# Attention on one core: scores and probabilities of two sequences in one step, and later products with v

## The chip, the core and the metric

The kernel runs on one core of a Trainium2 chip, in one launch. TensorE multiplies a stationary operand by a moving one into PSUM (eight banks of 128 partitions x 512 fp32), VectorE (DVE), ScalarE (ACT) and GpSimd (POOL) work beside it, and SyncE starts the DMAs. Each engine goes through its own queue in order and waits on semaphores. The metric is device time in microseconds. The kernel before takes 2264.89 us, the median of three runs (2263.42 to 2267.68).

## The reference

Four layers with residuals run over 16 sequences of 256 tokens, width 256: attention, a mixture of 16 experts (two per token) with shared ones, a state-space layer, a second mixture. Each layer's input and output are normalised, and the result is added to x. Only attention matters here. It has 16 query heads and 4 key/value heads of width 16, so that four query heads share one key head:

```
q = rope((x @ Wq.T + bq));  k = rope((x @ Wk.T + bk));  v = x @ Wv.T + bv
scores = q . k * 16**-0.5, causal mask
attended = softmax(scores) @ v
out = attended @ Wo.T + bo
```

All of it is fp32.

## The kernel before, in words

The kernel's parts follow each other: attention for all 16 sequences, then the first mixture, then a tail of state-space layer and second mixture. In attention a sequence is two tiles of 128 tokens. Key head g lies in partitions 32g to 32g+15 (a slot of 32, `SLOT`), so the products of different key heads use different groups of 32 rows of TensorE's array.

Scores are computed twice. In `scores`, queries are the stationary operand and keys are the moving one; VectorE takes each query's negated maximum from PSUM (line 1325) and writes it beside q as a seventeenth column. q with that column is transposed again (`turn_m`), and in `probs` the keys are stationary and 4 x 128 queries move: this gives scores less their maximum, keys on partitions. ScalarE takes the exponential (line 1251). In `av` the v of one key head, with a column of ones for the sum, is stationary with 32 columns, and lands in partitions 32g to 32g+31 of bank 4 or 5. ScalarE copies this (`copy_av`), TensorE turns it (`turn_av`), VectorE divides (`att`), TensorE turns (`turn_att`) and multiplies with Wo (`proj`), and VectorE adds the bias, normalises and adds to x (`post`, line 1343).

Each of scores, probs and av is cut into six units (`unit(i)`, line 1036): a pair of key heads, by query tile and key tile, (0,0), (1,0), (1,1). Scores of query tile 1 see both key tiles in one unit, so a score unit has eight products of 128 keys or four of 256. A mask comes first into the same bank, as a bf16 product with all 128 rows (lines 1141 and 1171). Unit i of scores and of probs uses banks 0 and 1 or 2 and 3, by its heads; they alternate. An fp32 product shows as two records, one for each of its two passes.

The order is written out by hand: `ORDER` (line 1044) lists steps as (sequence ahead, step, index), and every engine goes through the same list by `go_through` (line 57) and does what is its own in each step. Bank 6 serves x, q-k-v and the turned output, bank 7 q and k, bank 4 the output product as well. On VectorE, `norm` waits for GpSimd's power of -0.5 (line 1393) and then normalises x itself (line 1290); `rope` (line 1293) reads q-k-v from PSUM with the bias, rotates, writes q in four adds (line 1315) and copies v (line 1319).

Line 1752 (ScalarE, scale and shift by column operands, 128x256) and line 1950 (GpSimd, 128x512 sum in fp32) are of the tail and serve as measures.

Of the kernel before, what the change touches and what calls it, by code (L numbers as in the profile page):

```python
# [16 lines left out]
ALU = mybir.AluOpType  # L17
# [3 lines left out]
P = 128  # L21
# [892 lines left out]
class Attention:  # L914
# [8 lines left out]
    def __init__(self, k, a):  # L923
# [18 lines left out]
        self.qm_ready = k.sem("attn_qm_ready")  # L942
# [28 lines left out]
    def buffers(self, sb):  # L971
# [22 lines left out]
        self.probs = sb("probs", [P, 2, SEQ_TILES, REP, P])  # L994
# [33 lines left out]
SEQS = B  # L1028
# [7 lines left out]
def unit(i):  # L1036
# [17 lines left out]
def attention_order(t, par, first, last):  # L1054
    for ahead, what, i in ORDER:
        if not (ahead == -1 and first or ahead == 1 and last):
            yield what, t + ahead, (par + ahead) % 2, i


def attention_head(self):  # L1060
    for what, i in (("norm", 0), ("turn_x", 0), ("qkv", 0), ("rope", 0), ("qkv", 1), ("rope", 1),
                    ("turn_q", 0), ("turn_q", 1), ("turn_k", 0)):
        yield what, 0, 0, i
    yield from attention_order(0, 0, True, False)
    yield from attention_order(1, 1, False, False)


def attention_pair(self, it):
    yield from attention_order(2 * it + 2, 0, False, False)
    yield from attention_order(2 * it + 3, 1, False, False)  # L1070


def attention_rest(self):
    yield from attention_order(SEQS - 2, 0, False, False)
    yield from attention_order(SEQS - 1, 1, False, True)
    for what, i in (("turn_av", 1), ("att", 0), ("turn_att", 0), ("proj", 0), ("post", 0)):
        yield what, SEQS - 1, 1, i
# [3 lines left out]
Attention.turns = (SEQS - 4) // 2  # L1081
# [3 lines left out]
def is_last(t, n):  # L1085
    return isinstance(t, int) and t == n - 1


def attention_tensor(k, m, pe):
    nc = k.nc  # L1090

    def step(what, t, par, i):
        qb, half, heads = unit(i)
        if what == "turn_x":
            pe.wait_ge(m.xn_ready, t + 1)
            if begun(t - 1):
                pe.wait_ge(m.attT_ready, t - 1)
            for c in range(KD):
                for j in range(SEQ_TILES):
                    last = nc.tensor.transpose(k.bank[:, 6, (c * SEQ_TILES + j) * P:(c * SEQ_TILES + j + 1) * P],  # L1100
                                               m.xn[:, j, c * P:(c + 1) * P], k.ident[:])
            last.then_inc(m.xT_full, 1)
        if what == "qkv":
            pe.wait_ge(m.xT_ready, t + 1)
            if begun(2 * t + i):
                pe.wait_ge(m.qkv_read, 2 * t + i)
            for c in range(KD):
                last = nc.tensor.matmul(k.bank[:, 6, 0:NQKV], m.xT[:, c, i * P:(i + 1) * P], m.w_qkv[:, c, :],  # L1108
                                        start=(c == 0), stop=(c == KD - 1))
            last.then_inc(m.qkv_full, 1)  # L1110
        if what == "turn_q":
            pe.wait_ge(m.rope_ready, 2 * t + i + 1)
            if i == 0:
                if begun(2 * t):
                    pe.wait_ge(m.qmT_ready, 2 * t)
            else:
                pe.wait_ge(m.qkv_read, 2 * t + 2)
            for r in range(REP):
                last = nc.tensor.transpose(k.bank[:, 7 - i, r * P:(r + 1) * P],
# [1254 lines left out]
```

## Time and profile before

| | |
|---|---|
| median of three runs | 2264.89 us |
| the profiled execution's own time | 2262.32 us |
| its span | 2260.5 us |
| TensorE busy | 2044.2 us, 90% |
| VectorE, ScalarE, GpSimd busy | 1316.9, 740.8, 306.3 us |
| mean granted clock of TensorE | 0.944 |

Busy time of an engine is the time in which it executes something; matmuls are pipelined and their ends are modelled, so the distance from one start to the next says more than a duration. The granted clock is 1.00 at 2.4 GHz and 0.50 at 1.2 GHz; a mean between them says that part of the stretch ran at either. "Idle before" is the time an engine stood still before an instruction, with what ended it. A few matmul records are missing from a trace.

### The profile page before, as it was taken

The page shows a single profiled execution, that of the slowest core. Times are in us where ns is not written, and L with a number is a line of the kernel's source. Part 1 is how long each engine was busy: PE and PEld are TensorE (multiplying, and loading weights), DVE is VectorE, ACT ScalarE, POOL GpSimd, SP SyncE. Part 2 cuts the span into 40 slices and gives each one's busy share as a digit, 9 for nine tenths or more (in the row PEclk, how much of TensorE's full clock was granted, in tenths as well). Part 3 has the DMA queues.
Part 4 walks back from the last instruction along what each step waited for, and adds up shares of the span by engine and source line. Part 5 has one row for each costly group of instructions (what it writes and reads, how often), then busy time and mean ns, then how long its engine had stood idle before and what let it go on. Part 6 is the DMA issues. An engine that isn't in the chain of part 4 may idle for free.

```text
span 2260.5 us, 34928 instructions
## 1 busy us (share of the span) xinstructions
PE 2044.2 (90%) x10162; PEld 1455.7 (64%) x10211; DVE 1316.9 (58%) x3916; ACT 740.8 (33%) x1495; POOL 306.3 (14%) x459
## 2 busy tenths in 40 slices
PE   7999999997689888885579999999999999999998
PEld 3544454443667655553367887778777787777887
DVE  3565655553533222223667777777777777777653
ACT  1233323332234322322433443334333343333321
POOL 1000000001055333333000010011100011000000
PEclk7899989988599999998779999999999999999999
DMA  9800000000022222223111101111011110111100
GB/s 347 159 1 0 0 0 0 0 0 1 0 81 93 76 77 77 74 77 143 66 52 52 57 6 56 56 52 56 5 56 56 52 45 16 56 56 38 43 20 32
DMA packets 75462, 120.74 MB, mean 53 GB/s; under 512 B 18420, under 2 KB 59508, under 8 KB 74868
## 3 DMA queue, kind: packets, MB, share of 16 engines
q1 hardware_dynamic: 68468, 100.93, 14.1%
q0 software_dynamic: 6912, 18.92, 2.3%
q8 instruction: 28, 0.46, 0.1%
q14 instruction: 54, 0.44, 0.1%
HBM read 81.73 MB, written 38.08 MB: 53 GB/s over the span
## 4 chain that ended last, share of the span: by engine, by line
PE 77%; DVE 9%; issue 6%; DMA 4%; ACT 3%; POOL 1%; SPq 0%; DVEq 0%; POOLq 0%; ACTq 0%
PE bank L184 20%; PE bank L193 10%; PE bank L1146 5%; PE bank L1175 5%; DMA moe_rows<-sorted_in 3%; PE bank L561 3%; PE bank L1185 3%; PE bank L617 2%; PE bank L1624 2%; PE bank L1108 2%; DVE conv L1845 2%; PE bank L579 2%; PE bank L637 2%; PE bank L524 2%; PE bank L1212 2%
## 5 line engine op out<-in xcount | busy, mean ns | idle before, releaser
L184 PE MATMUL bank<-moe_xT,up_w 128*128 128x256 f32 x2304 | 552.3, 383 | 0.0
L184 PEld LDWEIGHTS bank<-moe_xT,up_w 128*128 128x128 f32 x2304 | 433.9, 190 | 69.7 <-issue 11.4
L193 PE MATMUL bank<-down_w,moe_hT 128*128 128x256 f32 x1152 | 306.5, 389 | 34.0 <-ACT moe_y L230 18.4
L227 ACT ACTIVATE moe_silu<-bank 128x256 f32<-128x256 f32 x288 | 110.7, 384 | 636.2 <-PE bank L184 636.2
L193 PEld LDWEIGHTS bank<-down_w,moe_hT 128*128 128x128 f32 x1152 | 203.9, 190 | 74.2 <-issue 28.8
L1325 DVE TENSOR_REDUCE q_slots<-bank 128x4 f32<-128x1024 f32 (+1 forms) x96 | 116.3, 1221 | 124.9 <-PE bank L1146 124.9
L1251 ACT ACTIVATE probs<-bank 128x1024 f32<-128x1024 f32 x96 | 98.4, 1025 | 201.8 <-PE bank L1175 201.8
L617 PE MATMUL bank<-up_w,moe_xT 128*128 x320 | 114.5, 481 | 25.9 <-issue 25.3
L1146 PE MATMUL bank<-kT,qT 16*128 16x256 f32 (+1 forms) x1024 | 124.9, 376 | 0.0
L1866 DVE TENSOR_TENSOR_SCAN m<-bank,delta 128x256 f32<-128x256 f32 x128 | 86.6, 676 | 61.8 <-PE bank L1663 60.5
L824 DVE TENSOR_TENSOR moe_h<-moe_silu,bank 128x176 f32<-128x176 f32 x80 | 27.0, 337 | 152.6 <-ACT moe_silu L696 149.9
L294 DVE TENSOR_TENSOR moe_hT<-moe_silu,bank 128x256 f32<-128x256 f32 x256 | 107.7, 421 | 8.8
L1175 PE MATMUL bank<-qmT,kT 17*128 17x512 f32 x384 | 110.9, 654 | 0.0
L293 DVE TENSOR_TENSOR moe_silu<-moe_silu,up_w 128x256 f32<-128x256 f32 x192 | 81.1, 422 | 43.3 <-ACT moe_silu L227 37.4
L1146 PEld LDWEIGHTS bank<-kT,qT 16*128 16x128 f32 x1024 | 83.3, 204 | 35.0 <-issue 30.1
L637 PE MATMUL bank<-down_w,moe_hT 88*128 x320 | 89.3, 401 | 0.6 <-ACT moe_hT L701 0.6
L561 PE MATMUL bank<-up_w,moe_xT 128*128 128x352 f32 x256 | 88.4, 469 | 0.9 <-issue 0.5
L617 PEld LDWEIGHTS bank<-up_w,moe_xT 128*128 128x128 f32 x320 | 55.6, 194 | 51.8 <-issue 35.4
L868 POOL DMA_INDIRECT results<-moe_result,moe_home x80 | 79.4, 993 | 20.1 <-POOL pool_spare L867 14.9
L326 POOL TENSOR_TENSOR moe_prstd<-moe_pmv,minus_half 128x2 f32<-128x2 f32 x16 | 12.4, 773 | 514.0 <-DVE moe_pmv L304 514.0
L1845 DVE SCALAR_TENSOR_TENSOR conv<-feat,taps,conv 128x256 f32<-128x256 f32 x192 | 80.0, 478 | 0.6
L1185 PE MATMUL bank<-probs,v_slots 128*32 128x512 f32 x384 | 75.8, 606 | 0.3
(293 smaller groups left out, 3226.9 us busy)
## 6 DMA issues: line engine op xcount, KB each, us to landing
up_w<-comb_rows SPq DMA_DIRECT2D x32, 768.0 KB, 5.2
comb_got<-results SPq DMA_DIRECT2D x16, 768.0 KB, 7.8
moe_rows<-sorted_in SPq DMA_DIRECT2D x80, 128.5 KB
sorted_in<-zero SPq DMA_DIRECT2D x10, 1024.0 KB, 10.3
down_w<-comb_rows SPq DMA_DIRECT2D x16, 512.0 KB, 7.6
up_w<-in_up SPq DMA_DIRECT2D x2, 3168.0 KB, 14.5
up_w<-in_up SPq DMA_DIRECT2D x2, 2304.0 KB, 13.0
results<-moe_y SPq DMA_DIRECT2D x32, 128.0 KB
```

Of the source, the lines that this page charges most:

```text
L184: last = mm(k.bank[:, UP_BANK + i % 3, half * S:(half + 1) * S], m.w_up[:, c, at + half * m.inter:at + (half + 1) * m.inter], m.xT[:, par, ...
L193: last = mm(k.bank[:, SUM_BANK, j * D:(j + 1) * D], m.hT[:, i % 3, j * P:(j + 1) * P], m.w_down[:, m.expert(i), :], start=(i == 0 and j == ...
L227: nc.scalar.activation(m.silu[:, i % 3, :], k.bank[:, UP_BANK + i % 3, 0:S], ACT.Silu).then_inc(m.silu_ready, 1)
L294: tt(m.hT[:, i % 3, :], m.silu[:, i % 3, :], u, ALU.mult).then_inc(m.h_ready, 1)
L561: last = nc.tensor.matmul(k.bank[:, 2 + i, 0:2 * inter], m.xT[:, par, c, :], m.w_up[:, c, lo:lo + 2 * inter], start=(c == 0), stop=(c == K ...
L617: last = nc.tensor.matmul(k.bank[:, 2 + par, 0:2 * inter], m.xT[:, par, c, :], cols(m.w_up[:, c, :], expert, 2 * inter), start=(c == 0), s ...
L637: last = nc.tensor.matmul(k.bank[:, 6 + par, 0:D], m.hT[0:m.half, par, c, :], w_down[0:m.half, bass.ds(expert * 2 * D + c * D, D)], start= ...
L1146: last = nc.tensor.matmul(x[:, r, :], m.qT[rows, par, qb, half * per + r, :], m.kT[rows, par, 0:keys], start=False, stop=(r == per - 1), s ...
L1175: last = nc.tensor.matmul(k.bank[:, g, :], m.kT[rows, par, half * P:(half + 1) * P], m.qmT[rows, qb].rearrange("p r n -> p (r n)"), start= ...
L1185: last = nc.tensor.matmul(k.bank[OW * g:OW * (g + 1), 4 + qb, :], m.v[:, par, half, g, :], m.probs[:, i % 2, g % PAIR].rearrange("p r n -> ...
L1325: v.tensor_reduce(m.q[:, par, qb, half * per:(half + 1) * per, heads[0]:heads[0] + PAIR, HD].rearrange("p r g -> p g r"), k.bank[:, heads[ ...
L1845: last = stt(dst, src[:, i:i + S], taps[:, i:i + 1], dst, ALU.mult, ALU.add)
```

## The change

One step, `pair`, takes the place of `scores` and `probs`. In period t it does score unit i of sequence t+1 and probability unit i^1 of sequence t, so the two use different pairs of key heads and with them different groups of rows. Masks of both come first; then products alternate, score and probability, until the probability's two are issued, and the rest of the scores follow. Scores always use banks 0 and 1, probabilities 2 and 3, and the next `pair` waits for the maximum (`max_ready`) and the exponential (`probs_ready`) of the one before. `probs` has four buffers instead of two.

`av` has three steps of four products, two units each, one step after their exponentials; the third comes in the next period. q-k-v is computed two sequences ahead, x is normalised three ahead. The bias add with the read of PSUM is a step of its own (`read`), ahead of the rotation (`rope`). Bank 6 now takes the output product too, and each of banks 6 and 7 is used for one thing at a time, with waits for its last reader. ScalarE normalises x (`xn`) and the output (`z`) by scale and shift and copies v (`copy_v`); GpSimd computes the shift with two small instructions and adds the output to x (`add`); VectorE takes that sum's statistics in a later step (`stat`). VectorE writes q by one add over all heads, and divides in one instruction per tile. The loop runs over (16 - 6) / 2 turns of two periods, with three periods and the preparation of sequences 0 and 1 ahead of it and six behind.

```diff
-        self.probs = sb("probs", [P, 2, SEQ_TILES, REP, P])
+        self.probs = sb("probs", [P, 4, PAIR, REP, P])
+        self.shift = sb("attn_shift", [P, SEQ_TILES])
+        self.pshift = sb("attn_pshift", [P, SEQ_TILES])
...
+SCORE_BANK, PROB_BANK, AV_BANK, MIX_BANK, TURN_Q_BANK = 0, 2, 4, 6, 7
 ORDER = (
-    (0, "scores", 0), (0, "scores", 1), (0, "scores", 2), (0, "turn_m", 0), (-1, "att", 0), (-1, "turn_av", 1),
-    (0, "scores", 3), (0, "scores", 4), (-1, "turn_att", 0), (1, "norm", 0), (0, "scores", 5), (-1, "proj", 0),
-    (0, "probs", 0), (-1, "post", 0), (1, "turn_x", 0), (0, "probs", 1), (0, "turn_m", 1), (1, "qkv", 0),
-    (0, "av", 0), (0, "probs", 2), (1, "rope", 0), (0, "av", 1), (0, "copy_av", 0), (0, "probs", 3), (1, "qkv", 1),
-    (0, "av", 2), (0, "av", 3), (0, "probs", 4), (0, "turn_av", 0), (1, "rope", 1), (1, "turn_q", 0), (0, "probs", 5),
-    (1, "turn_k", 0), (1, "turn_q", 1), (0, "av", 4), (0, "av", 5), (0, "copy_av", 1),
+    (0, "pair", 0), (1, "scores", 0), (0, "probs", 0), (1, "copy_v", 0), (3, "norm", 0), (-1, "av", 2), (-1, "copy_av", 1),
+    (0, "turn_m", 1), (2, "qkv", 0), (2, "read", 0),
+    (0, "pair", 1), (1, "scores", 1), (0, "probs", 1), (-1, "turn_av", 1), (-1, "att", 0), (3, "xn", 0), (2, "qkv", 1),
+    (2, "read", 1), (-2, "z", 0), (-2, "add", 0),
+    (0, "pair", 2), (1, "scores", 2), (0, "probs", 2), (0, "av", 0), (0, "copy_av", 0), (-1, "turn_att", 0), (1, "turn_m", 0),
+    (2, "rope", 0),
+    (0, "pair", 3), (1, "scores", 3), (0, "probs", 3), (0, "turn_av", 0), (3, "turn_x", 0), (2, "turn_q", 0), (2, "rope", 1),
+    (0, "pair", 4), (1, "scores", 4), (0, "probs", 4), (0, "av", 1), (2, "turn_q", 1), (-2, "stat", 0),
+    (0, "pair", 5), (1, "scores", 5), (0, "probs", 5), (-1, "proj", 0), (-1, "post", 0), (2, "turn_k", 0),
...
+def attention_period(t, par):
     for ahead, what, i in ORDER:
-        if not (ahead == -1 and first or ahead == 1 and last):
+        here = (0, 1) if what == "pair" else (ahead,)
+        if not isinstance(t, int) or any(0 <= t + a < SEQS for a in here):
             yield what, t + ahead, (par + ahead) % 2, i
...
+        if what == "pair":
+            scores, probs = within(t + 1), within(t)
+            if scores:
+                s, its = t + 1, (par + 1) % 2
+                qb, half, heads = unit(i)
+                keys, per = (qb + 1) * P, REP // (qb + 1)
+                pe.wait_ge(m.qT_ready, 2 * s + qb + 1)
+                pe.wait_ge(m.kT_ready, s + 1)
+                if begun(UNITS * s + i):
+                    pe.wait_ge(m.max_ready, UNITS * s + i)
+                for n in range(PAIR):
+                    x = k.bank[:, SCORE_BANK + n, :].rearrange("p (r n) -> p r n", r=per)
+                    mm(x[:, :, keys - P:keys], k.ident_b[:], m.mask_q[:, 0:per, :], start=True, stop=False,
+                       skip_group_check=True)
+            if probs:
+                pqb, phalf, pheads = unit(i ^ 1)
+                masked = phalf == pqb
+                pe.wait_ge(m.qmT_ready, 2 * t + pqb + 1)
+                if begun(UNITS * t + i):
+                    pe.wait_ge(m.probs_ready, UNITS * t + i)
+                if masked:
+                    for n in range(PAIR):
+                        mm(k.bank[:, PROB_BANK + n, :], k.ident_b[:], m.mask_k[:].rearrange("p r n -> p (r n)"),
+                           start=True, stop=False, skip_group_check=True)
+            for n in range(PAIR * REP):
+                r, lane = divmod(n, PAIR)
+                if scores and r < per:
+                    rows = slice(SLOT * heads[lane], SLOT * heads[lane] + HD)
+                    last = mm(k.bank[:, SCORE_BANK + lane, r * keys:(r + 1) * keys], m.qT[rows, its, qb, half * per + r, :],
+                              m.kT[rows, its, 0:keys], start=False, stop=(r == per - 1), skip_group_check=True)
+                    if n == PAIR * per - 1:
+                        last.then_inc(m.scores_full, 1)
+                if probs and r == 0:
+                    rows = slice(SLOT * pheads[lane], SLOT * pheads[lane] + HD + 1)
+                    last = mm(k.bank[:, PROB_BANK + lane, :], m.kT[rows, par, phalf * P:(phalf + 1) * P],
+                              m.qmT[rows, pqb].rearrange("p r n -> p (r n)"), start=not masked, stop=True,
+                              skip_group_check=True)
+                    if lane == PAIR - 1:
+                        last.then_inc(m.probs_full, 1)
...
+            pe.wait_ge(m.probs_ready, UNITS * t + PAIR * i + PAIR)
+            qb, half, _ = unit(PAIR * i)
             if i == 0:
+                pe.wait_ge(m.v_ready, t + 1)
                 if begun(t):
-                    pe.wait_ge(m.proj_used, t)
-            for g in heads:
-                last = nc.tensor.matmul(k.bank[OW * g:OW * (g + 1), 4 + qb, :], m.v[:, par, half, g, :],
-                                        m.probs[:, i % 2, g % PAIR].rearrange("p r n -> p (r n)"),
-                                        start=(half == 0), stop=(half == qb), skip_group_check=True)
+                    pe.wait_ge(m.att_ready, t)
+            for u in (PAIR * i, PAIR * i + 1):
+                for g in unit(u)[2]:
+                    last = mm(k.bank[OW * g:OW * (g + 1), AV_BANK + qb, :], m.v[:, par, half, g, :],
+                              m.probs[:, ((u ^ 1) + 2 * par) % 4, g % PAIR].rearrange("p r n -> p (r n)"),
+                              start=(half == 0), stop=(half == qb), skip_group_check=True)
             last.then_inc(m.probs_used, 1)
...
+        if what == "xn":
+            act.wait_ge(m.rstd_ready, t + 1)
+            if begun(t):
+                act.wait_ge(m.xT_full, t)
+            for j in range(SEQ_TILES):
+                last = activation(m.xn[:, j, :], cols(k.x, SEQ_TILES * t + j), ACT.Identity, bias=m.shift[:, j:j + 1],
+                                  scale=m.rstd[:, j:j + 1])
+            last.then_inc(m.xn_ready, 1)
...
+        if what == "read":
+            dve.wait_ge(m.qkv_full, 2 * t + i + 1)
+            if i == 0 and begun(t):
+                dve.wait_ge(m.v_ready, t)
+            v.tensor_tensor(m.qkv[:, i, :], k.bank[:, MIX_BANK, 0:NQKV], m.b_qkv[:], ALU.add).then_inc(m.qkv_read, 1)
...
-            for g in range(KV):
-                sl = slice(g * REP * HD, (g + 1) * REP * HD)
-                v.tensor_tensor(m.q[:, par, i, :, g, 0:HD], m.rot_a[:, sl].rearrange("p (r f) -> p r f", r=REP),
-                                m.rot_b[:, sl].rearrange("p (r f) -> p r f", r=REP), ALU.add)
+            v.tensor_tensor(m.q[:, par, i, :, :, 0:HD].rearrange("p r g f -> p g r f"),
+                            m.rot_a[:, 0:NQ].rearrange("p (g r f) -> p g r f", g=KV, r=REP),
+                            m.rot_b[:, 0:NQ].rearrange("p (g r f) -> p g r f", g=KV, r=REP), ALU.add)
             v.tensor_tensor(m.kk[:, i, :, 0:HD], m.rot_a[:, NQ:NQK].rearrange("p (g f) -> p g f", g=KV),
-                            m.rot_b[:, NQ:NQK].rearrange("p (g f) -> p g f", g=KV), ALU.add)
-            v.tensor_copy(m.v[:, par, i, :, 0:HD], m.qkv[:, i, NQK:NQKV].rearrange("p (g f) -> p g f", g=KV))\
-                .then_inc(m.rope_ready, 1)
+                            m.rot_b[:, NQ:NQK].rearrange("p (g f) -> p g f", g=KV), ALU.add).then_inc(m.rope_ready, 1)
...
+        if what == "add":
+            pool.wait_ge(m.z_ready, t + 1)
+            x = cols(k.x, t, SEQ_TILES * D)
+            g.tensor_tensor(x, x, m.y[:].rearrange("p j d -> p (j d)"), ALU.add).then_inc(m.x_done, 1)
```

## Rows read from the trace of the kernel before

**Rows 1.** The page's first block: busy time, share, instructions of each engine

```profile
PE 2044.2 (90%) x10162; PEld 1455.7 (64%) x10211; DVE 1316.9 (58%) x3916; ACT 740.8 (33%) x1495; POOL 306.3 (14%) x459
```

**Rows 2.** Windows: us, busy (count) per engine, clock, DMA, GB/s

```profile
24.30:64.10 39.80, 39.31 (x164) 18.31 (x166) 13.85 (x34) 9.78 (x13) 0.70 (x1) 0.66 1.07 338
...
139.66:170.09 30.43, 30.06 (x181) 14.99 (x183) 18.82 (x57) 10.77 (x15) 1.39 (x2) 1.00 0.00 1
...
291.80:326.01 34.21, 33.84 (x181) 17.06 (x183) 19.43 (x57) 10.77 (x15) 1.39 (x2) 0.88 0.00 0
326.01:360.67 34.66, 34.12 (x181) 17.30 (x183) 18.89 (x56) 10.77 (x15) 1.39 (x2) 0.87 0.00 0
```

**Rows 3.** Timeline, TensorE, 170 to 202: start us, us, line, count, idle

```profile
171.96 1.99 PE L1212 MATMUL bank<-w_o,attT 128*128 128x256 f32 x8
...
177.45 0.66 PE L1157 MATMUL bank<-ident,q_slots 128*128 128x128 f32 x4
177.94 1.46 PE L1108 MATMUL bank<-w_qkv,attn_xT 128*128 128x384 f32 x4
179.33 1.05 PE L1185 MATMUL bank<-probs,v_slots 128*32 128x512 f32 x4
180.31 1.13 PE L1175 MATMUL bank<-qmT,kT 17*128 17x512 f32 x4
...
184.89 1.07 PE L1185 MATMUL bank<-probs,v_slots 128*32 128x512 f32 x8
186.12 0.38 PE L1171 MATMUL bank<-mask_k,ident_b 128*128 128x512 bf16 x1 [0.16 <-issue]
...
188.42 0.59 PE L1171 MATMUL bank<-mask_k,ident_b 128*128 128x512 bf16 x2
188.94 1.13 PE L1175 MATMUL bank<-qmT,kT 17*128 17x512 f32 x4
190.00 0.44 PE L1126 MATMUL bank<-ident,k_slots 128*128 128x128 f32 x2
...
190.80 1.44 PE L1185 MATMUL bank<-probs,v_slots 128*32 128x512 f32 x8
192.18 0.60 PE L1141 MATMUL bank<-mask_q,ident_b 128*128 128x512 bf16 x2
...
194.34 1.16 PE L1146 MATMUL bank<-kT,qT 16*128 16x128 f32 x16
195.43 0.39 PE L1141 MATMUL bank<-mask_q,ident_b 128*128 128x256 bf16 x2
195.75 1.13 PE L1146 MATMUL bank<-kT,qT 16*128 16x256 f32 x8
196.83 0.66 PE L1157 MATMUL bank<-ident,q_slots 128*128 128x128 f32 x4
```

**Rows 4.** Groups of VectorE, 170.09 to 200.52: count, busy us, mean ns, idle

```profile
L1325 DVE TENSOR_REDUCE q_slots<-bank 128x4 f32<-128x1024 f32 x5 | 6.0, 1216 | 0.2 <-PE bank L1146 0.2
...
L1315 DVE TENSOR_TENSOR q_slots<-rot_a,rot_b 128x64 f32<-128x64 f32 x8 | 1.3, 220 | 0.1
...
L1358 DVE TENSOR_SCALAR attn_y<-attn_y,attn_pmv,attn_prstd 128x256 f32<-128x256 f32 x2 | 0.7, 412 | 0.8 <-POOL attn_prstd L1396 0.8
```

**Rows 5.** Groups of ScalarE, same stretch; last row whole span

```profile
L1251 ACT ACTIVATE probs<-bank 128x1024 f32<-128x1024 f32 x6 | 6.1, 1024 | 11.4 <-PE bank L1175 11.4
...
L1752 ACT ACTIVATE conv<-feat,taps 128x256 f32<-128x256 f32 x64 | 33.0, 589 | 0.0
```

**Rows 6.** Groups of GpSimd, whole span

```profile
L1950 POOL TENSOR_TENSOR down_w<-down_w 128x512 f32<-128x512 f32 x16 | 20.2, 1264 | 254.7 <-ACT down_w L1771 254.7
```

**Rows 7.** Timeline, TensorE, 314 to 320

```profile
314.42 1.16 PE L1146 MATMUL bank<-kT,qT 16*128 16x128 f32 x16
...
317.46 1.74 PE L1146 MATMUL bank<-kT,qT 16*128 16x256 f32 x8
```

**Rows 8.** Timeline, all engines, the stage's start

```profile
23.79 0.59 PE L1141 MATMUL bank<-mask_q,ident_b 128*128 128x512 bf16 x2 [0.82 <-ACT kT L1239]
```

**Rows 9.** Timeline, all engines, the stage's end

```profile
554.30 0.22 DVE L712 TENSOR_TENSOR moe_diff<-next_stat 128x32 f32<-128x32 f32 x1
```

More of the change, by code:

```diff
@@ L1051 @@
 )
-def attention_order(t, par, first, last):
+def attention_period(t, par):
     for ahead, what, i in ORDER:
-        if not (ahead == -1 and first or ahead == 1 and last):
+        here = (0, 1) if what == "pair" else (ahead,)
+        if not isinstance(t, int) or any(0 <= t + a < SEQS for a in here):
             yield what, t + ahead, (par + ahead) % 2, i
 def attention_head(self):
[L1061 to L1065, printed above, removed]
+    for s in (0, 1):
+        for what, i in (("norm", 0), ("xn", 0), ("turn_x", 0)):
+            yield what, s, s, i
+        if s == 0:
+            for what, i in (("qkv", 0), ("read", 0), ("qkv", 1), ("read", 1), ("rope", 0), ("rope", 1), ("turn_q", 0), ("turn_q", 1), ("turn_k", 0)):
+                yield what, s, s, i
+    for t in (-1, 0, 1):
+        yield from attention_period(t, t % 2)
@@ L1080, with within @@
 Attention.head, Attention.pair, Attention.rest = attention_head, attention_pair, attention_rest
-Attention.turns = (SEQS - 4) // 2
+Attention.turns = (SEQS - 6) // 2
 Attention.finished = SEQS
-def is_last(t, n):
-    return isinstance(t, int) and t == n - 1
+def within(t):
+    return not isinstance(t, int) or 0 <= t < SEQS
 def attention_tensor(k, m, pe):
     nc = k.nc
+    mm, turn = nc.tensor.matmul, nc.tensor.transpose
     def step(what, t, par, i):
-        qb, half, heads = unit(i)
+        mix, turned = k.bank[:, MIX_BANK, :], k.bank[:, TURN_Q_BANK, :]
@@ L1152, in step @@
             if i == 0:
-                pe.wait_ge(m.kT_ready, t + 1)
+                if begun(t):
+                    pe.wait_ge(m.qmT_ready, 2 * t)
+                else:
+                    pe.wait_ge(m.kT_ready, 1)
             else:
                 pe.wait_ge(m.qmT_ready, 2 * t + 1)
+                if within(t + 1):
+                    pe.wait_ge(m.kT_ready, t + 2)
             for r in range(REP):
-                last = nc.tensor.transpose(k.bank[:, 7, r * P:(r + 1) * P],
-                                           m.q[:, par, i, r].rearrange("p g s -> p (g s)"), k.ident[:])
+                last = turn(turned[:, r * P:(r + 1) * P], m.q[:, par, i, r].rearrange("p g s -> p (g s)"), k.ident[:])
@@ L1192, in step @@
             for r in range(REP):
-                last = nc.tensor.transpose(k.bank[:, 4 + i, r * P:(r + 1) * P], m.avT[:, i, r, :], k.ident[:])
+                last = turn(k.bank[:, AV_BANK + i, r * P:(r + 1) * P], m.avT[:, i, r, :], k.ident[:])
             last.then_inc(m.av_turned, 1)
@@ L1262, in step @@
                 act.wait_ge(m.proj_full, t)
-            nc.scalar.copy(m.attT[:].rearrange("p c t -> p (c t)"), k.bank[:, 6, :]).then_inc(m.attT_ready, 1)
+            copy(m.attT[:].rearrange("p c t -> p (c t)"), mix).then_inc(m.attT_ready, 1)
+        if what == "z":
+            act.wait_ge(m.post_rstd, t + 1)
+            for j in range(SEQ_TILES):
+                last = activation(m.y[:, j, :], m.y[:, j, :], ACT.Identity, bias=m.pshift[:, j:j + 1],
+                                  scale=m.prstd[:, j:j + 1])
+            last.then_inc(m.z_ready, 1)
     go_through(m, act, step)
```

206 lines of the change are left out of this document (84 added, 122 removed).

## The prediction

> **What bounds the kernel now.** I read the page's first block, then a table of stretches, one for each sequence of the attention stage, then TensorE's timeline inside one sequence, then the groups of the other engines there. TensorE is busy for 90% of the span [rows 1]. The change touches only the attention stage, which ends where the expert layer's first vector instruction starts, at 554.30 us [rows 9]. In the stretches the reader is to see that one sequence takes 30.43 us at full clock, that TensorE is busy in 30.06 of them, and that VectorE has 18.82 and ScalarE 10.77 [rows 2]. So TensorE's order of work alone sets the pace, and sixteen sequences of it are the stage.
>
> What fills it is in the timeline. I use start to start, since shown durations overlap. A probability product (two heads, 17 rows of the array each, 512 columns) takes 188.94 to 190.00 = 1.06 us. A score product (two heads, 16 rows each) takes 1.09 or 1.08 us, 128 or 256 keys wide [rows 3]. Two row groups of four work in each, the other two idle. With v, two column groups work in the first unit's product: 179.33 to 180.31, 0.98. The row at 184.89 shows eight records, two units at once in four column groups. The next row starts 1.23 later, but it holds one mask where there are two, a record is missing; less one mask (0.215) the four groups took about 1.0, as two do. So one pass over the array costs about 1.05 us however many groups are in it; for columns the trace shows that, for four row groups it doesn't.
>
> The clock is the second cost. The sequences that start at 291.80 and 326.01 took 34.21 and 34.66 instead of 30.43, with a granted clock of 0.88 and 0.87 [rows 2]: together 8.0 us. The two from 421.52 lose the same 8 (34.24, 34.64 in the same view). Before the first fall the engine did the two 128-key score products with their masks, only 16-row work; the fall shows as 1.74 for a group [rows 7] that takes 1.13 elsewhere [rows 3].
>
> **The change part by part.** *Mixed steps.* Six score stages and six probability stages a sequence become six stages with both, scores on one pair of row groups, probabilities on the other (the index i^1 sees to that). Masks stay as many. If four row groups overlap as four column groups do, each of the six saves one stage: 1.06 and the entry after the masks, which is 188.42 to 188.94 less two masks of 0.215, so 0.09 [rows 3]; 1.15 x 6 = 6.9. Bounds per mixed stage: 1.09 (full overlap) and 1.09 + 1.06 = 2.15 (none); below 1.09 it can't go, since the score half alone takes that. I take 1.09: the column rows are the nearest, and both kinds use the same size of row group, so nothing has to switch between them.
>
> The rule that speaks against this is in the Trainium skill, page "TensorE: Matmul & The Clock Gate", Part 3: four row tiles with 512 columns gave 3.07 times the speed, not 4. By it a full stage would be 4/3.07 x 1.06 = 1.38, an estimate, and the sum 26 us longer (0.29 x 90 stages). No row here has four row groups, so the trace neither agrees nor disagrees.
>
> *Products with v.* Six steps become three of four column groups. Two pairs ran together already, one did not: 0.98 saved.
>
> *Waits that go.* The last pair of products with v takes 190.80 to 192.18, 1.38 where its like takes 1.0: it waits for its exponential, and one step later it won't. 0.38 saved. New period: 30.43 - 6.9 - 0.98 - 0.38 = 22.17.
>
> *Waits that come.* Scores now have banks 0 and 1 alone, probabilities 2 and 3. Mixed step n+1 waits for the maximum of step n (1.22 us on VectorE, first in its order) and for its exponential (1.02 on ScalarE) [rows 4, 5]; behind a waiting TensorE stands everything else. The cover is what TensorE does between: 2.9, 1.9, 2.0, 1.5, 1.5, 2.1 us in the six steps (transposes 0.49, q-k-v 1.39, output product 1.99, v 1.0, half a transpose group for k [rows 3]). The smallest, 1.5, is above 1.22 plus about 0.1 of signalling by 0.15. VectorE's tail in steps 2 and 3 is the rotation, about 1.65 without the bias add, after a 1.13 pitch of the maximum: 2.8 against TensorE's 3.4 and 2.85. It fits, narrowly, in step 3. I add 0.33 a period for small misses, twice that margin: 22.5.
>
> *Other engines.* VectorE loses two normalisations, 0.7 each, the residual add and the v copies, and eight adds of 64 columns (1.3 busy) become two of 256, the products with the reciprocals likewise [rows 4]: under 17 of 22.5. ScalarE gains four 128x256 scale-and-shift instructions and a copy; the nearest row is 589 ns [rows 5], so 2.4 + 0.4 on 10.77: 13.6 of 22.5. GpSimd gains the residual add, 1.26 by its nearest row [rows 6], and small ones; the add stands two steps ahead of the statistics that wait for it. All these cost nothing while TensorE sets the pace; bounds 0 to 1.3 a period, if the add and z came to lie ahead of TensorE.
>
> *Ends.* One sequence's scores are now alone at the front and one's probabilities at the back. The head does rotation after both bias adds and also turns x of sequence 1 ahead of the first scores: normalise 1.3, GpSimd 1.2, ScalarE 1.1, turn 1.1, estimates of mine from the same stage's durations at the slow clock, with 0.3 for the later rotation, on top of q and k at 23.79. First mask at 28.8 instead of 23.79 [rows 8]. The score-only period has 14.0 us of full-clock work (scores with masks 9.0, q-k-v 2.8, turns 2.2). TensorE was slow in most of the stretch from 24.30 to 64.10 (clock 0.66, so about 27 us at half) [rows 2]; I leave that as it is until 51.6: 11.4 lost, and 3 of waits. Period with probabilities alone: six times product and exponential in turn, about 16. Tail from the last product with v: about 16, as now, GpSimd's add in place of VectorE's.
>
> **The sum.** 28.8 + (14.0 + 3 + 11.4) + 15 x 22.5 + 16 + 16 = 426.7, against 554.3: 127.6 less. No fall of the clock is in it, because no stretch of 16-row work alone is left after the first period: mixed stages have twice the rows and denser work on both sides. The profiled execution took 2262.3 (span 2260.5 and 1.8 around it): 2134.7. The median of the runs is 2.6 above it: 2137.
>
> **The rivals.** *A, overlap in part.* The scores' later products might be held until the first of the two passes of a probability product is through: 0.53 + three quarters of 1.09 = 1.35 for 1.09. 90 times 0.26 is 23: 2160. For it: products of unlike length never ran together here. Against: two products of the four groups come from another step, and still all eight records fit in 1.0, so each group goes on by itself [rows 3]. The skill's 3.07 points the same way.
>
> *B, one set of banks.* The maximum comes late in the narrow steps, since it stands behind the rotation: four steps a period at 0.6, 15 periods: 36, so 2173. The Trainium skill, page "SBUF — State Buffer", section on who interferes with whom, has GpSimd hold up a VectorE instruction with two SBUF inputs; by that the 1.26 add would lengthen this path by at most 19 in all, an estimate. No row here shows it.
>
> *C, the mixture does nothing.* Row groups beyond two run one after the other: each mixed stage 2.15, 90 x 1.06 = 95 more: 2232. The row of eight records speaks against it, for columns.
>
> *D, slower.* Unlike products don't overlap at all. In the order score, probability, score, probability, each product counts in full, 1.06 and 1.09 less 0.2 of fill, the second in four: 0.85 + 0.22 + 0.85 + 0.22, then 0.67 for the other scores and 0.3 of entry = 3.1 in two steps, 3.3 in four. That is 12.9 a period more, 193 in all: 2330, slower by 65. It begins to lose where a mixed stage is over 1.09 + 128/90 = 2.5. Nothing in the profile is for it but that no such mixture is in it.
>
> *E, the clock.* Falls as before (8.0 each); one to three would give 2145 to 2161. With full clock in the first period it would be 11 less.
>
> **How the numbers follow.** The forecast (2117 to 2152, E's single fall in it) 0.62, A 0.13, B 0.15, C 0.05, D 0.03, and 0.02 for something near no gain. Time 2137. Range 2117 (period 21.9 and the first clock gained: -9, -11) to 2176 (B with a little over). This leaves out about 0.15. Faster by over 0.2% (4.5 us, about what a measurement of this kernel can tell from no change) 0.96, within 0.2% 0.01, slower 0.03.
>
> **What would show it.** Right: 22.5 us between one sequence's turned outputs and the next; one mixed stage of 1.1 us with score and probability records side by side; eight records with v in 1.0 at each of three places; granted clock 1.00 in all stretches after the first; attention over at about 427. A shows as mixed stages of 1.35, B as TensorE waiting for the maximum's line in steps 3 to 5, C as 2.15, D as over 2.5. The prediction is wrong if the period is over 25, or if time moves outside the attention stage by more than a few us.

## The result, and the profile after

The changed kernel takes 2133.31 us (median of 4 runs, 2132.08 to 2137.06) against 2266.28 (4 runs, 2263.42 to 2269.0) for the kernel before beside it: ratio 0.9422, 95% interval 0.9405 to 0.9439. The profiled execution took 2132.08 us (span 2130.3). The forecast was 2137, with 2117 to 2176 around it. Ratios compare fast executions only: one of run 12's twelve (2281.26 us) was over 1.5% above the fastest of its kernel and isn't in its ratio.

The page's first block of the changed kernel (busy us, share, instructions of each engine) answers to [rows 1]:

```profile
PE 1905.2 (89%) x10210; PEld 1422.4 (67%) x10211; DVE 1267.0 (59%) x3612; ACT 776.6 (36%) x1575; POOL 336.4 (16%) x539
```

TensorE's busy time fell by 139 us, and its share stayed about as it was. The same array work is done, more of it at once. In the windows view (start:end, us, then busy time and count of PE, PEld, DVE, ACT and POOL, granted clock, DMA share, GB/s) a steady sequence answers to [rows 2]; the first row is the score-only period, the second about the first mixed one:

```profile
27.52:51.50 23.98, 21.98 (x105) 12.76 (x104) 12.40 (x24) 4.59 (x9) 1.05 (x3) 0.64 1.03 399
51.50:74.35 22.85, 21.73 (x157) 12.30 (x155) 12.40 (x24) 10.81 (x16) 1.05 (x3) 0.86 1.16 220
...
222.00:244.78 22.78, 22.24 (x186) 13.39 (x182) 15.91 (x38) 12.99 (x21) 3.45 (x8) 1.00 0.00 0
```

The reader is to see 22.78 us where there were 30.43, TensorE still busy in all but half a microsecond, and VectorE, ScalarE and GpSimd with room left. TensorE's timeline (start, duration, line, operation, count, and in brackets the idle time before it with its releaser) has the start of a period, which answers to [rows 3]:

```profile
231.23 2.00 PE L1234 MATMUL bank<-w_o,attT 128*128 128x256 f32 x8
233.06 0.38 PE L1143 MATMUL bank<-ident,k_slots 128*128 128x128 f32 x2
233.99 0.60 PE L1157 MATMUL bank<-mask_q,ident_b 128*128 128x512 bf16 x2 [0.54 <-ACT kT L1271]
234.43 0.60 PE L1167 MATMUL bank<-mask_k,ident_b 128*128 128x512 bf16 x2
234.95 0.37 PE L1174 MATMUL bank<-kT,qT 16*128 16x128 f32 x1
234.96 0.69 PE L1180 MATMUL bank<-qmT,kT 17*128 17x512 f32 x1
234.97 0.37 PE L1174 MATMUL bank<-kT,qT 16*128 16x128 f32 x1
234.97 0.69 PE L1180 MATMUL bank<-qmT,kT 17*128 17x512 f32 x1
235.17 0.51 PE L1174 MATMUL bank<-kT,qT 16*128 16x128 f32 x6
235.49 0.59 PE L1180 MATMUL bank<-qmT,kT 17*128 17x512 f32 x1
...
236.05 1.06 PE L1208 MATMUL bank<-probs,v_slots 128*32 128x512 f32 x8
237.05 0.66 PE L1197 MATMUL bank<-ident,q_slots 128*128 128x128 f32 x4
```

Score (L1174) and probability (L1180) records stand side by side, and the whole mixed stage takes 234.95 to 236.05 = 1.10 us. A product is two records here, one behind the other. The eight products with v take 236.05 to 237.05 = 1.00. The one idle place is the first mask, 0.54 us, and it waits for ScalarE's copy of the turned k, not for a maximum. Waits from 100 to 372 us (us in total, times, longest) say the same:

```profile
PE bank L1157 <- ACT kT L1271: 5.4, 9, 0.7
...
PE bank L1157 <- DVE q_slots L1361: 0.5, 1, 0.5
```

The same timeline at the stage's front, and the timeline of all engines at its end, answer to [rows 8, 9]:

```profile
27.52 1.06 PE L1157 MATMUL bank<-mask_q,ident_b 128*128 128x512 bf16 x2
...
39.68 0.38 PE L1157 MATMUL bank<-mask_q,ident_b 128*128 128x256 bf16 x2 [0.83 <-DVE q_slots L1361]
...
50.89 1.01 PE L1157 MATMUL bank<-mask_q,ident_b 128*128 128x512 bf16 x2 [0.80 <-DVE q_slots L1361]
...
391.29 0.59 PE L1167 MATMUL bank<-mask_k,ident_b 128*128 128x512 bf16 x2
```

```profile
421.45 1.26 POOL L1438 TENSOR_TENSOR x<-x,attn_y 128x512 f32<-128x512 f32 x1 [1.20 <-ACT attn_y L1302]
422.74 0.75 DVE L1395 BATCH_NORM_STATS2 next_stat<-x 128x6 f32<-128x256 f32 x2 [3.72 <-POOL x L1438]
423.63 0.22 DVE L712 TENSOR_TENSOR moe_diff<-next_stat 128x32 f32<-128x32 f32 x1
```

The expert layer starts at 423.63 instead of 554.30: 130.7 us less. What lies behind it takes 1706.7 us of the span, against 1706.2. So all of the gain is in the attention stage.

### The profile page after: what moved, and what is told of

Read it like the earlier page. It is cut to its first block, busy times and chain, and to the rows that moved or that the text cites. A ratio compares the mean times of both kernels' runs of the same rounds, so it can differ in the third digit from the quotient of the medians.

```text
span 2130.3 us, 34947 instructions
## 1 busy us (share of the span) xinstructions
PE 1905.2 (89%) x10210; PEld 1422.4 (67%) x10211; DVE 1267.0 (59%) x3612; ACT 776.6 (36%) x1575; POOL 336.4 (16%) x539
## 4 chain that ended last, share of the span: by engine, by line
PE 75%; DVE 10%; issue 6%; DMA 4%; ACT 4%; POOL 1%; SPq 0%; DVEq 0%; POOLq 0%; ACTq 0%
PE bank L184 21%; PE bank L193 11%; PE bank L561 4%; DMA moe_rows<-sorted_in 4%; PE bank L1174 4%; PE bank L617 3%; PE bank L1666 3%; PE bank L1127 2%; DVE conv L1887 2%; PE bank L1208 2%; PE bank L637 2%; PE bank L579 2%; PE bank L524 2%; PE bank L1180 2%; PE bank L1644 2%
## 5 line engine op out<-in xcount | busy, mean ns | idle before, releaser
L184 PEld LDWEIGHTS bank<-moe_xT,up_w 128*128 128x128 f32 x2304 | 435.2, 191 | 68.5 <-issue 11.4
L193 PEld LDWEIGHTS bank<-down_w,moe_hT 128*128 128x128 f32 x1152 | 204.5, 190 | 73.7 <-issue 28.8
L1361 DVE TENSOR_REDUCE q_slots<-bank 128x4 f32<-128x1024 f32 (+1 forms) x96 | 117.7, 1226 | 107.1 <-PE bank L1174 107.1
L824 DVE TENSOR_TENSOR moe_h<-moe_silu,bank 128x176 f32<-128x176 f32 x80 | 27.0, 338 | 152.3 <-ACT moe_silu L696 152.3
L1174 PE MATMUL bank<-kT,qT 16*128 16x256 f32 (+1 forms) x1024 | 114.0, 351 | 0.0
L1180 PE MATMUL bank<-qmT,kT 17*128 17x512 f32 x384 | 109.8, 645 | 0.6 <-ACT probs L1286 0.6
L1174 PEld LDWEIGHTS bank<-kT,qT 16*128 16x128 f32 x1024 | 78.9, 192 | 37.1 <-issue 35.1
L803 DVE TENSOR_TENSOR moe_h<-moe_silu,bank 128x176 f32<-128x176 f32 x64 | 21.6, 338 | 85.2 <-ACT moe_silu L670 85.2
```

Of the source, the lines that this page charges most:

```text
L184: last = mm(k.bank[:, UP_BANK + i % 3, half * S:(half + 1) * S], m.w_up[:, c, at + half * m.inter:at + (half + 1) * m.inter], m.xT[:, par, ...
L193: last = mm(k.bank[:, SUM_BANK, j * D:(j + 1) * D], m.hT[:, i % 3, j * P:(j + 1) * P], m.w_down[:, m.expert(i), :], start=(i == 0 and j == ...
L1174: last = mm(k.bank[:, SCORE_BANK + lane, r * keys:(r + 1) * keys], m.qT[rows, its, qb, half * per + r, :], m.kT[rows, its, 0:keys], start= ...
L1180: last = mm(k.bank[:, PROB_BANK + lane, :], m.kT[rows, par, phalf * P:(phalf + 1) * P], m.qmT[rows, pqb].rearrange("p r n -> p (r n)"), st ...
L1361: v.tensor_reduce(m.q[:, par, qb, half * per:(half + 1) * per, heads[0]:heads[0] + PAIR, HD].rearrange("p r g -> p g r"), k.bank[:, SCORE_ ...
```

## The experiments

"Period" is from one sequence's turned outputs (the transposes of `att`, L1225) to the next, in steady state; the steps alternate by 0.1 us, so it is a mean of two. Each ratio is to the runs of the kernel before on the same chip.

**1. The changed kernel again.**

> The changed kernel once more, beside its own variants. All theories: 2133 us, sequence period 22.8 us, 0.5 us of each spent waiting for the copy of the turned k, no fall of the granted clock between the first mixed period and the last output product.

2136.11 us (2134.0 to 2140.61), ratio 0.9445 (0.9423 to 0.9467). Period 22.78 as before, attention over at 426.0. The first turned outputs stand at 87.9 us instead of 85.5, with the same code, and the profiled executions differ by about the same, 2.5 (2134.6 and 2132.08). The difference is there before the first mask: x is turned 0.5 later, and the second q-k-v product takes 2.90 instead of 1.53.

**2. Scores and probabilities on the same pair of row groups.** The edit takes the overlap away and leaves all else.

```diff
-                pqb, phalf, pheads = unit(i ^ 1)
+                pqb, phalf, pheads = unit(i)
...
-                              m.probs[:, ((u ^ 1) + 2 * par) % 4, g % PAIR].rearrange("p r n -> p (r n)"),
+                              m.probs[:, (u + 2 * par) % 4, g % PAIR].rearrange("p r n -> p (r n)"),
```

> In each mixed step the probabilities are of the same pair of key heads as the scores, so both use the same two groups of rows; all else as in the changed kernel. Theory: the gain is the overlap of four row groups; without it a mixed stage takes 2.15 instead of 1.1 us, 6 x 1.05 x 15 = 95 more, 2228, the size of the forecast's case C. Rival: the gain is fewer entries and waits, and row groups matter little: under 2150. For the clock: if it falls in stretches of 16- and 17-row work alone, it will fall again here, 8 us each on top.

2227.77 us (2224.57 to 2232.12), ratio 0.9853 (0.9831 to 0.9875). Period 27.9, 5.1 more. TensorE's timeline of one of its stages:

```profile
244.42 0.71 PE L1174 MATMUL bank<-kT,qT 16*128 16x256 f32 x4
244.96 1.03 PE L1180 MATMUL bank<-qmT,kT 17*128 17x512 f32 x4
245.82 0.60 PE L1174 MATMUL bank<-kT,qT 16*128 16x256 f32 x4
246.35 1.99 PE L1234 MATMUL bank<-w_o,attT 128*128 128x256 f32 x8
```

The stage takes 1.93 instead of about 1.09, with the two kinds one behind the other; 0.84 x 6 = 5.0 is the period's difference. The version is 92 us slower than run 1 (2227.77 less 2136.11). Not all of that is overlap: 90 stages at 0.84 are 76. The traces' attention stages end 93.8 apart (519.8 and 426.0), and the other 18 lie where the clock stood at half in this trace and not in run 1's: 1.5 in the sequence from 318.6 us and most of the rest from 455 us on. All four executions have a lower mean clock than run 1's five, 0.942 to 0.945 against 0.948 to 0.953. Whether the falls come of the edit isn't shown. So about 76 of the 133 us gained are shown to hang on the `i ^ 1`.

**3. Each four-group product with v cut in two**, with transposes between the halves.

```diff
-    (0, "pair", 2), (1, "scores", 2), (0, "probs", 2), (0, "av", 0), (0, "copy_av", 0), (-1, "turn_att", 0), (1, "turn_m", 0),
+    (0, "pair", 2), (1, "scores", 2), (0, "probs", 2), (0, "ava", 0), (-1, "turn_att", 0), (0, "avb", 0), (0, "copy_av", 0), (1, "turn_m", 0),
...
```

> Each of the three products with v of a period is cut in two halves of two column groups with a group of transposes between them. Theory: a half costs as much as the whole, 0.98 each, three a period: 16 x 2.9 = 47 more, 2180. Rival: a half costs half, no change but 0.1 us for more entries: 2138.

2181.33 us (2180.76 to 2182.06), ratio 0.9648 (0.9632 to 0.9664). Period 26.14, 3.36 more. Its timeline:

```profile
244.69 1.05 PE L1208 MATMUL bank<-probs,v_slots 128*32 128x512 f32 x4
245.68 0.66 PE L1226 MATMUL bank<-ident,att 128*128 128x128 f32 x4
246.26 1.05 PE L1208 MATMUL bank<-probs,v_slots 128*32 128x512 f32 x4
247.25 0.66 PE L1197 MATMUL bank<-ident,q_slots 128*128 128x128 f32 x4
```

Half the records take 0.99, as all eight do, so four column groups cost what two do; three times 0.99 is 2.97. Part of the other 0.39 is entries: the transposes at 245.68 take 0.58 to the next start, where such a group takes 0.49.

**4. Scale and shift, and the addition to x, back on VectorE.**

```diff
+        if what == "xn":
+            dve.wait_ge(m.rstd_ready, t + 1)
...
+            for j in range(SEQ_TILES):
+                last = v.tensor_scalar(m.xn[:, j, :], cols(k.x, SEQ_TILES * t + j), m.mv[:, j, 0:1],
+                                       m.rstd[:, j:j + 1], ALU.subtract, ALU.mult)
...
+        if what == "add":
+            dve.wait_ge(m.z_ready, t + 1)
+            x = cols(k.x, t, SEQ_TILES * D)
+            v.tensor_tensor(x, x, m.y[:].rearrange("p j d -> p (j d)"), ALU.add).then_inc(m.x_done, 1)
```

> Normalising x, normalising the output and the residual add are back on VectorE, at their places in the new order; the rest as in the changed kernel. Theory: VectorE then has 5.1 us in the second step against TensorE's 3.9, the maximum of the third step comes late, and TensorE waits 1.1 to 2 us a period: 16 to 30 more, 2150 to 2163. Rival: TensorE's slack takes it, since VectorE stays under 20 of 22.8 us: 2133.

2149.77 us (2149.59 to 2157.99), ratio 0.9507 (0.9491 to 0.9523). Period 24.05, 1.27 more. VectorE's timeline, and TensorE's, in step 2:

```profile
254.77 0.72 DVE L1340 TENSOR_SCALAR attn_y<-attn_y,attn_pmv,attn_prstd 128x256 f32<-128x256 f32 x2
255.64 0.69 DVE L1346 TENSOR_TENSOR x<-x,attn_y 128x512 f32 x1 [0.15 <-DVE attn_y L1340]
256.25 1.22 DVE L1379 TENSOR_REDUCE q_slots<-bank 128x4 f32<-128x1024 f32 x1
```

```profile
257.53 0.39 PE L1157 MATMUL bank<-mask_q,ident_b 128*128 128x256 bf16 x2 [1.14 <-DVE q_slots L1379]
```

The maximum starts when the addition ends, and TensorE's next mask starts when the maximum ends. This is rival B's mechanism in one place. VectorE is far from full, and still 1.4 us in the wrong step cost 1.1. So the margin of this step is thin, and it is the moved instructions that keep it.

**5. k turned ahead of the output product**, so that ScalarE's copy has 2 us of cover.

```diff
-    (0, "pair", 5), (1, "scores", 5), (0, "probs", 5), (-1, "proj", 0), (-1, "post", 0), (2, "turn_k", 0),
+    (0, "pair", 5), (1, "scores", 5), (0, "probs", 5), (2, "turn_k", 0), (-1, "proj", 0), (-1, "post", 0),
```

> The transposes of k stand ahead of the output product instead of behind it. Theory: what is left above the summed period is the wait of the next period's first mixed step for ScalarE's copy of the turned k (0.54 us of 22.78); the output product now covers it, so the period goes to 22.2 and the whole to 2133 - 15 x 0.54 = 2125. Rival: the wait for the maximum of the last scores stands right behind it, then only 0.1 to 0.2 us a period go, 2131.

2127.45 us (2121.49 to 2137.0), ratio 0.9404 (0.9376 to 0.9431). Windows and timeline:

```profile
222.00:243.97 21.97, 21.97 (x188) 13.36 (x182) 15.86 (x37) 12.83 (x20) 3.40 (x7) 1.00 0.00 0
```

```profile
250.73 0.44 PE L1143 MATMUL bank<-ident,k_slots 128*128 128x128 f32 x2
251.00 1.89 PE L1234 MATMUL bank<-w_o,attT 128*128 128x256 f32 x8
252.73 0.60 PE L1157 MATMUL bank<-mask_q,ident_b 128*128 128x512 bf16 x2
```

TensorE is busy in all of the period, which is 0.81 shorter: the wait was real, and no other took its place. The gain is 0.27 more than the 0.54 of idle time shown, since k's transposes and the output product together now take 2.00 to the next mask (250.73 to 252.73) where they took 2.76 with the wait (231.23 to 233.99). Yet the stage is over only 5.2 us earlier than in run 1, where twelve periods and more should give 10. The last two periods are 20.52 and 14.95 against 18.88 and 12.98, with the clock at half in pieces from 371.6 us on. So 3.6 of the gain was given back in the thin last periods. Over medians the gain on run 1 is 8.7 us, with six runs spread over 15 and intervals that just overlap (0.9431 against 0.9423): the period is shown shorter, the whole time only nearly so.

**6. As 5, and x of sequence 1 normalised and turned during q-k-v of sequence 0.**

```diff
-    for s in (0, 1):
-        for what, i in (("norm", 0), ("xn", 0), ("turn_x", 0)):
-            yield what, s, s, i
+    for what, s, i in (("norm", 0, 0), ("xn", 0, 0), ("turn_x", 0, 0), ("qkv", 0, 0), ("read", 0, 0), ("norm", 1, 0),
+                       ("xn", 1, 0), ("qkv", 0, 1), ("read", 0, 1), ("turn_x", 1, 0), ("rope", 0, 0), ...
```

> As the run with k turned earlier, and sequence 1 is normalised and turned during the q-k-v products of sequence 0. Theory: the first mask moves from 27.5 to about 25 us and all behind it: 2.5 less, 2122. Rival: at the slow clock the first periods are set by the clock's own times, and a start 2.5 us earlier meets a longer slow stretch: between -4 and +4 about 2125.

2126.31 us (2117.99 to 2127.37), ratio 0.9383 (0.9360 to 0.9406): the lowest median here, and clear of run 1. In the traces the stage ends 1.9 us before that of run 5 (418.9), all of it from the head (first mask at 27.57 instead of 29.43); the two intervals overlap, so as a time the 1.9 isn't shown.

**7. All score products issued ahead of the probabilities.**

```diff
+            for n in range(PAIR * REP):
+                r, lane = divmod(n, PAIR)
                 if probs and r == 0:
```

> In each mixed step all score products are issued first, then the two probability products; same work. Theory 1 (TensorE starts products in the order of the program, each as soon as its row group is free): the probabilities start only when the last scores have started, 0.65 us later in the two 128-key steps and 0.43 later in the four 256-key steps, 3.0 us a period, 15 x 3.0 = 45: 2178. Theory 2 (each row group has its own queue and nothing waits for another's): no change, 2133.

2147.71 us (2146.93 to 2153.42), ratio 0.9490 (0.9465 to 0.9514). Period 23.78, 1.0 more. Neither theory holds as it was put. The 128-key stages are dearer, the 256-key ones (254.72 to 255.81 = 1.09) are not:

```profile
245.65 0.83 PE L1174 MATMUL bank<-kT,qT 16*128 16x128 f32 x10
246.22 0.70 PE L1182 MATMUL bank<-qmT,kT 17*128 17x512 f32 x2
246.31 0.50 PE L1174 MATMUL bank<-kT,qT 16*128 16x128 f32 x6
246.75 0.59 PE L1182 MATMUL bank<-qmT,kT 17*128 17x512 f32 x2
247.27 0.64 PE L1210 MATMUL bank<-probs,v_slots 128*32 128x512 f32 x4
```

Ten score records start before the first of the probabilities, 0.57 us later than the scores, and the stage takes 1.62.

**8 to 10. Probabilities first; four scores first; six scores first.**

```diff
-            for n in range(PAIR * REP):
+            for kind, n in [("s", n) for n in range(6)] + [("p", 0), ("p", 1)] + [("s", n) for n in range(6, PAIR * REP)]:
...
```

This is run 10's line; runs 8 and 9 have the two `"p"` ahead of all eight and behind four.

> The changed kernel with both probability products issued ahead of all score products in every mixed stage. It asks what the first rearrangement (all scores first, 2148, about 0.5 us dearer in each of the two 128-key stages of a period and nothing in the four 256-key stages) means. Theory 'short look-ahead': TensorE's queue runs in order but starts work for another pair of row groups as long as it is not too far behind the head; only two products stand ahead of the scores here, so the mixed stage stays at 1.10, the period at 22.78 and the time at 2133 to 2136. Rival 'strict start': scores begin only when the second probability product has begun its second pass: 0.5 us more in all six stages, 3.0 a period, 2180.

> The changed kernel with four score products issued ahead of the two probability products, and the other four of a 128-key stage behind them. The 256-key stages then have the order of the kernel with all scores first. Theory 'short look-ahead': four score products (two for each of their row groups) do not hold the probabilities back: period 22.78, 2133 to 2136. Rival 'any product ahead costs its share': half of what eight cost, 0.25 us in each of two stages, 0.5 a period, about 2141.

> As the kernel with four scores first, but six ahead. Theory 'short look-ahead': the point at which the probabilities are held lies between four and eight products; if the queue past which TensorE sees holds four, the two more products (0.14 us each by the 1.09 us that eight take in two row groups) delay them by 0.27, twice a period: 0.5, about 2141. If it holds six: 2135. Rival, eight are special (the masks or the end of the stage): no cost, 2135; so 2141 against 2135.

Probabilities first: 2141.94 us (2134.14 to 2145.64), ratio 0.9472 (0.9455 to 0.9490), period 22.82, stage 237.04 to 238.14 = 1.10. The period is as expected, so the rival falls; the median is 6 above what I expected, the profiled execution took 2134.14, and what the others lost no trace shows. Four first: 2135.46 (2130.18 to 2138.16), ratio 0.9431 (0.9412 to 0.9449), period 22.72: no cost. Six first: 2143.97 (2141.98 to 2147.04), ratio 0.9480 (0.9464 to 0.9497), period 23.34. The 128-key stage with six, then with four ahead:

```profile
238.53 0.60 PE L1174 MATMUL bank<-kT,qT 16*128 16x128 f32 x6
238.86 0.70 PE L1180 MATMUL bank<-qmT,kT 17*128 17x512 f32 x2
238.96 0.61 PE L1174 MATMUL bank<-kT,qT 16*128 16x128 f32 x8
239.40 0.59 PE L1180 MATMUL bank<-qmT,kT 17*128 17x512 f32 x2
```

```profile
236.26 0.38 PE L1174 MATMUL bank<-kT,qT 16*128 16x128 f32 x2
236.29 0.70 PE L1180 MATMUL bank<-qmT,kT 17*128 17x512 f32 x2
236.47 0.61 PE L1174 MATMUL bank<-kT,qT 16*128 16x128 f32 x8
```

Four products are 8 records, and the probabilities start after 2 of them; of 12 they wait for 6, of 16 for 10. Each time six records stand ahead that have not started. That number fits three lengths; what holds it in the chip these runs don't show. They do show that the description ahead of the prediction, each engine goes through its queue in order, is too strict for TensorE: in run 7 the probabilities start at 246.22 and 0.09 us later six records start that were issued ahead of them.

**11, 12. The kernel before, with its two 128-key score products parted by a transpose**, run in two jobs.

```diff
-    (0, "scores", 0), (0, "scores", 1), (0, "scores", 2), (0, "turn_m", 0), (-1, "att", 0), (-1, "turn_av", 1),
+    (0, "scores", 0), (-1, "turn_av", 1), (0, "scores", 1), (0, "scores", 2), (0, "turn_m", 0), (-1, "att", 0),
```

> The kernel before with one move: the transposes of the second attended tile stand between the first two score units instead of behind the third; same work. Theory: the clock falls where both 128-key score units and their masks run with nothing dense between; broken up, the two late falls (8.0 us each) go: 2266 - 16 = 2250, with a granted clock of 1.00 in all sequences after the first three. Rival: the falls come from something else and stay: 2266.

> The kernel before with its two 128-key score products broken up by a transpose step, once more, for its trace: in the first trace of it the clock fell in every period from 197 us on, and its time was the longest of its six. Theory 'it varies between executions': an execution near the median of 2247 shows two falls fewer than the kernel before and periods of 30.8 at full clock. Rival 'the edit costs elsewhere and the clock falls in each execution': the same falls every period, and a time near 2247 all the same.

First 2247.5 us (2244.8 to 2275.02, 6 runs), ratio 0.9937 (0.9921 to 0.9954); then 2263.54 (2244.47 to 2281.26, 12 runs), ratio 0.9971 (0.9941 to 1.0001). The 18 times lie in three clumps: nine from 2244 to 2249, five from 2263 to 2266, four from 2274 to 2282. Both profiled executions came from the slowest clump. Two sequences of the second, by windows:

```profile
194.65:225.35 30.70, 30.64 (x184) 14.96 (x183) 18.84 (x57) 10.76 (x15) 1.38 (x2) 1.00 0.00 0
257.84:291.82 33.98, 33.92 (x184) 16.65 (x182) 19.03 (x57) 10.76 (x15) 1.38 (x2) 0.90 0.00 0
```

The same work takes 30.70 and 33.98, by the clock alone, and most sequences of that trace after 227 us are of the second kind. The mean granted clock goes with the clumps: 0.953 to 0.960 in the first, 0.946 to 0.952 in the second, 0.939 to 0.941 in the third. So the same code has executions with many falls and others with fewer. Parting the two products is no cure: the 14.5 us by which the first median lay below the kernel before weren't there in the second job. No trace of an execution from the lowest clump was taken, and which work makes the clock fall stays open.

## Why the prediction was right

**The mixed stage**, its largest term: 1.09 us for score and probability together, 6.9 a period. Measured 1.10, 1.10, 1.08, 1.07 in the stages from 234.95, 239.79, 242.98 and 249.59. Run 2 shows that the row groups are the cause, since with the same work on one pair a stage takes 1.93. The inference from column groups to row groups held.

**Rival A** (1.35, 2160) falls for this order of issue. The Trainium skill's 3.07 for four row tiles (page "TensorE: Matmul & The Clock Gate", Part 3, on the measured speedup) would have made a stage 1.38, the prediction's estimate; the trace has 1.10 against 1.06 for two groups, so four groups give nearly twice two. But runs 7 and 10 show that A's idea, a product held up by what was issued ahead of it, isn't empty. It costs 0.5 a stage with eight scores ahead, and the kernel's alternation avoids it; I had not seen that the order of issue carried a condition.

**Rival C** (2232) put the price of no overlap at 2.15 a stage. The changed kernel's 1.10 refutes the mechanism. Its price was too high as well: run 2 has 1.93, since its four probability records take 0.86 from their start to the next scores (244.96 to 245.82), where they take 1.06 alone. That the whole time of run 2, 2228, came so near 2232 and the expected 2228 is luck: the 19 us that the stages cost less were made up by about 18 of slow clock. **Rival D** falls with the 1.10.

**Products with v**: 0.98 and 0.38 saved. Three stages of 1.00 without idle time stand in the trace, and run 3 gives the same price from the other side.

**The period**: 22.17 and 0.33 for small misses, 22.5; measured 22.78. The sum of the work was right to 0.2 (run 5's period without any wait is 21.97). The allowance was named wrongly: I watched the maximum in steps 3 to 5, and in the steady periods TensorE doesn't wait there. It waits once a period, 0.54 to 0.70, for ScalarE's copy of k, which is turned last in step 5 and needed first in step 0. The prediction listed that transpose group as cover of the maximum and didn't ask who reads it. Rows could have told: the wait for kT stood in [rows 8] already.

**Rival B** doesn't show in the steady periods, and its mechanism is real: run 4 produces it with 1.4 us of VectorE work. It also acts in the changed kernel itself, in the last mixed period, where there is no q-k-v left to cover the maximum:

```profile
378.03 0.38 PE L1157 MATMUL bank<-mask_q,ident_b 128*128 128x256 bf16 x2 [0.94 <-DVE q_slots L1361]
384.28 0.38 PE L1157 MATMUL bank<-mask_q,ident_b 128*128 128x256 bf16 x2 [0.90 <-DVE q_slots L1361]
387.65 0.38 PE L1157 MATMUL bank<-mask_q,ident_b 128*128 128x256 bf16 x2 [0.49 <-DVE q_slots L1361]
```

These are 2.3 us, once. The addition on GpSimd at 1.26 us [rows 6] is 1.26 to 1.28 here too. It runs beside the maximum (221.43 and 221.51 us), which reads only PSUM and takes 1226 ns (L1361) where it took 1216 before [rows 4]; the rotation's products start when the addition is nearly over, at 222.66. So these rows don't test the prediction's 19 us, which was for a VectorE instruction with two SBUF inputs.

**The ends.** From first mask to the first mixed period I had 28.8 to 57.2; measured 27.52 to 50.89. The head's extra work was put 1.3 too high, and the score-only period 5 too high: less time at the slow clock (about 8 lost instead of 11.4, by the granted clock of 0.64), 2.0 of waits instead of 3, and 0.8 less work. The 15 mixed periods then took 340.4 instead of 337.5, since the wait for k counts in most of them and the clock stayed low until 58.1. From 391.29 on it took 32.3 for 32. Together -6.3 + 2.9 + 0.3 = -3.1: 423.6 for 426.7. The hit is better than the steps under it: two misses of opposite sign.

**The clock, and rival E.** I counted no fall after the first periods and 16 us as regained from that. In the changed kernel's trace no fall stands between 58 and 413 us, and none stands between 64 and 369 us in runs 1 and 3 to 10 either. Run 2, in which two row groups idle again, has some (3.4 us at half from 335.5, longer ones from 455). The reason given was that no stretch of 16-row work alone is left. These rows don't carry it. The stretch ahead of the fall in [rows 7] wasn't of 16-row work alone, since the masks use all 128 rows; run 2, with two row groups at a time, held the full clock from 64 to 335 us; and in runs 5, 6 and 10 the clock fell inside the last mixed period (371.6, 369.7 and 385 us), where all four groups are in use. Runs 11 and 12 vary so much between executions of one code that one trace each doesn't show the cause. So the absence of falls was forecast rightly, and 16 us of the gain rest on it, but its reason isn't shown. The Trainium skill (page "TensorE: Matmul & The Clock Gate", Part 1) ties the lower of the two clock levels, 1.2 GHz, to TensorE's idleness. Here the clock also fell in sequences in which TensorE was busy in 33.92 of 33.98 us, so a row of busy time doesn't tell whether it will hold.

## What to carry to other kernels

Small products that left row groups or column groups empty cost as much here as full ones: pair them with products of another step that need the other groups, and put few products of one kind in a row, alternating the kinds (here four in a row cost nothing, six and eight did). When such a pairing shortens the period, ask of each last instruction of a step who reads it first in the next; here that, and not the engine with the most work, was the next 0.8 us. And when a change is worth less than a fall of the clock (8 us here), one profiled execution and four times can point the wrong way.

## What the runs showed of the hardware

- Four row groups, two with 16 rows and up to 256 columns a product and two with 17 rows and 512 columns, ran together in 1.07 to 1.10 us, where two take 1.06 to 1.09.
- A product for free row groups starts ahead of earlier ones that wait for theirs, as long as no more than six records stand between: a delay of 0.03 us with 8 score records issued ahead, 0.33 with 12, 0.57 with 16.
- The granted clock fell to half while TensorE was busy throughout, and its mean varied between executions of one kernel (run 12: 0.941 to 0.960, with times from 2275 to 2244 us).
